# New orders of steps for a fused attention and mixture-of-experts layer, and one wait of TensorE moved

## What is computed

```
xn = layernorm(x)
s  = attention(xn)          # 16 heads of 8; 4 heads causal over all keys, 12 over a window of 32
y  = sum over 16 experts of act(xn) * cw @ Wd, plus one shared expert of width 128
g  = silu(xn + y)           # cw: top 4 of 16 experts, out of 2 of 4 groups, by sigmoid of xn @ gate_w
out = x + s * g
```

## Time and profile before

| | |
|---|---|
| median of three runs | 529.96 us |
| profiled execution, its time | 530.82 us |
| its span (first to last instruction) | 529.0 us |
| PE busy | 480.5 us (91%) |
| DVE busy | 340.3 us (64%) |
| ACT busy | 330.3 us (62%) |
| POOL busy | 265.9 us (50%) |

### The profile page before, as it was taken

The page is one execution under the profiler, slowest core; times in us unless marked ns, Lnnn a source line. Parts: engine busy times, 40 slices in busy tenths (PEclk is TensorE's granted clock), DMA queues, the critical chain, the costliest instruction groups (busy, mean ns, idle before and its releaser), DMA issues.

```text
span 529.0 us, 10545 instructions
## 1 busy us (share of the span) xinstructions
PE 480.5 (91%) x3804; PEld 289.0 (55%) x3832; DVE 340.3 (64%) x755; ACT 330.3 (62%) x654; POOL 265.9 (50%) x239
## 2 busy tenths in 40 slices
PE   1969988999999988999999998999999987989995
PEld 0756655555457655555446765555456755544442
DVE  6876464885687555777588474877588532686415
ACT  3456744767957544666957546566967556266972
POOL 3227851265736952155745972155744962016623
PEclk9979998999999999999999999999999999899999
DMA  9256383000350575000360396000260187000001
GB/s 216 80 164 115 58 103 64 1 1 2 124 76 0 165 96 82 1 1 1 93 109 0 91 162 89 2 0 1 82 119 2 48 156 97 2 2 0 1 1 40
DMA packets 144077, 32.37 MB, mean 61 GB/s; under 512 B 120966, under 2 KB 136346, under 8 KB 144026
## 3 DMA queue, kind: packets, MB, share of 16 engines
q1 hardware_dynamic: 143696, 31.41, 30.2%
q10 hardware_dynamic: 330, 0.30, 0.3%
HBM read 22.25 MB, written 9.44 MB: 60 GB/s over the span
## 4 chain that ended last, share of the span: by engine, by line
PE 72%; DVE 9%; ACT 6%; issue 6%; SPq 2%; POOL 2%; DMA 1%; POOLq 1%; DVEq 0%; ACTq 0%
PE bank L791 10%; PE bank L739 7%; PE bank L678 6%; PE bank L572 6%; PE bank L574 6%; PE bank L573 6%; PE bank L708 5%; DVE mxp L1176 4%; PE bank L755 4%; PE bank L779 3%; ACT stage L936 2%; PE bank L690 2%; PE bank L720 2%; PE bank L646 2%; PE bank L662 1%
## 5 line engine op out<-in xcount | busy, mean ns | idle before, releaser
L936 ACT ACTIVATE stage<-bank 128x512 f32<-128x512 f32 (+3 forms) x240 | 112.5, 528 | 62.0 <-PE bank L720 32.2
L1253 POOL TENSOR_TENSOR wrow<-wrow,gates 128x512 f32<-128x512 f32 x64 | 82.1, 1283 | 97.1 <-ACT wrow L865 96.9
L1176 DVE TENSOR_REDUCE mxp<-bank 128x1 f32<-128x512 f32 (+4 forms) x192 | 90.3, 518 | 41.1 <-PE bank L681 32.8
L1262 POOL TENSOR_TENSOR hid<-hid,wrow 128x512 f32<-128x512 f32 x64 | 81.8, 1278 | 37.1 <-DVE hid L1140 31.9
L1140 DVE SCALAR_TENSOR_TENSOR hid<-hid,bank 128x512 f32<-128x512 f32 x72 | 48.7, 680 | 60.0 <-PE bank L574 39.9
L791 PE MATMUL bank<-hid,down_w 128*128 128x512 f32 x144 | 77.8, 629 | 0.0
L854 ACT ACTIVATE hid<-bank 128x512 f32<-128x512 f32 x72 | 43.3, 602 | 51.1 <-PE bank L574 50.9
L1245 POOL TENSOR_TENSOR maxd<-mxp,k 128x512 f16<-128x512 f32 x32 | 33.4, 1048 | 79.7 <-DVE mxp L1176 45.7
L678 PE MATMUL bank<-kall,qpad 128*128 128x512 f16 (+4 forms) x192 | 54.0, 331 | 12.6 <-issue 6.8
L572 PE MATMUL bank<-xh,up_hi 128*128 128x512 f32 x144 | 58.3, 405 | 0.0
L708 PE MATMUL bank<-kpad,kall 128*128 128x512 f16 (+3 forms) x192 | 55.3, 330 | 2.0 <-ACT stage L936 0.6
(11 more groups left out here) (158 smaller groups left out, 884.4 us busy)
## 6 DMA issues: line engine op xcount, KB each, us to landing
planes<-qkh SPq DMA_DIRECT2D x16, 256.0 KB, 3.1
qtmp<-planes SPq DMA_DIRECT2D x16, 256.0 KB, 3.2
kall<-planes SPq DMA_DIRECT2D x16, 256.0 KB, 3.5
qpad<-planes SPq DMA_DIRECT2D x128, 32.0 KB, 2.9
kpad<-planes SPq DMA_DIRECT2D x48, 64.0 KB, 3.3
xin<-in_L_attn_x_dram SPq DMA_DIRECT2D x4, 512.0 KB, 4.6
planes<-qkl SPq DMA_DIRECT2D x8, 256.0 KB, 3.0
xres<-in_L_attn_x_dram SPq DMA_DIRECT2D x4, 512.0 KB, 4.1
```

The lines of the kernel that those rows point to most:

```text
L936: act.activation(prob[:, t % NPROB, 0:cols], ps[:, 0:cols], ACT.Exp).then_inc(freed, 1)
L1176: ins = dve.tensor_reduce(mxp[:, c, j:j + 1], ps[:, 0:cols], AX_X, ALU.max)
L1253: pool.tensor_tensor(row, row, gates[:], ALU.mult).then_inc(gated, 1)
L1262: pool.tensor_tensor(hid[:, i % NHID, :], hid[:, i % NHID, :], wrow[:, (EP * c + t) % NWT, :] if t < EP else gates[:], ALU.mult)\
```

## The change

The three strings are replaced; each has as many of every letter as before. And PE's wait for `k32` moves from the step `small` to a place ahead of FIRST, since `small` is no longer PE's first step. No instruction is added or taken away but that wait.

```diff
-FIRST_ORDER = ("IPIPIPPIPIITTPIIPTTTPPVITTPIVIITTIXXXXIVPPPVPPVXXVPXXIXPVPPVXPXXVVXXX")
+FIRST_ORDER = ("PPIPPIPIIPPTITIPITTIIIITTIVPTPVTTPXXVVVXXVIXIVPXPXIXXPVPPPPPVPXVXXXXX")
...
                     elif kind == "small":
-                        pe.wait_ge(k32_loaded, 16)
                         pe.wait_ge(small_loaded, 5 * 16)
...
+            pe.wait_ge(k32_loaded, 16)
             sections(pe, walk)
```

More of the change, by code:

```diff
@@ L151, in expert_steps @@
     return out
-FIRST_ORDER = ("IPIPIPPIPIITTPIIPTTTPPVITTPIVIITTIXXXXIVPPPVPPVXXVPXXIXPVPPVXPXXVVXXX")
[L155 to L161, removed]
+FIRST_ORDER = ("PPIPPIPIIPPTITIPITTIIIITTIVPTPVTTPXXVVVXXVIXIVPXPXIXXPVPPPPPVPXVXXXXX")
+BODY_ORDER = ("AAAXRRRXAPRXXXAAAAAAAXRXAAARARPRAAXAAAAARXAXRRRRRAAAAARRRAAAAAAAARAAAAAAXAAAXRRRRXAPRAXXAAAARRRA"
+              "AAAARAAXRRARARARRRARAAAXXRARRRARRAPRAAXARRRRRXRRAAPAXAAXRRRRRXAAARRRRRRAAXRAPPAXRRPRXRRRXRXRTRRR"
+              "RRPRRTPRRRRRXRRTXRRRXXRPRRRRXRXRRRRRPPTRCTRXTXRRRRXRXCRRPRXTPRRRRPPRRRRRRRRXRXXPRRRRRXRTTRPCXXVX"
+              "V0XVC0VXVXVXV1V1VXXP0X1VXXXXX")
+LAST_ORDER = ("AAXXARRRRRAXAXXAARRXAARAAAARAXAXAAARRARAARRXAAAARARRAAAAAAAAAAAAAAXAAAXARAXRRRAAXARARRARARRAAAAA"
+              "RXAXARAARARARARRRRAARRAAAARXAAXARAXARXARAXAAAXAARRRRRRRXRRRXRRRRRRRRAAXRXRXRRXRRRRXXRRRRRRRRRRRX"
+              "RCRRRXRRRRRRCRRRRXRRRRRRRRXRRRRRRXRRXRRRRRRRRRRRRRRRRRXRXXX0XCCX0X1X011")
 FIRST_EXPERTS = expert_steps(0) + [("z", 0), ("z2", 0)]
```

## The result

The changed kernel takes 534.99 us (median of 20 runs, 531.30 to 538.55), the kernel before 530.99 in the runs beside it. It is slower by 4.0 us in the medians, within the 1% that was called "the same". The ratio of the runs beside each other is 1.0093, 95% interval 1.0071 to 1.0115; it is not that of the two medians and makes 3.8 to 6.1 us. Ratios leave out executions in the chip's slower state, of which there is one of `kpads12_act_old_head` and one of the kernel before. 533.3 was forecast. The profiled execution took 534.31 us with a span of 532.5, against 530.82 and 529.0.

The account below looks back on a forecast made before the run. PE is busy for 91% of the span, so only its waits and clock can change the time; `cwT`'s start sets FIRST's end. Span 529.0 + 4.0 (FIRST) - 0.7 (LAST) = 532.3, carried to the median 533.3 us; range 526.5 to 537.5.

Parts of the forecast that it names:

- Load and `gate`: Start of FIRST: `x` lands 0.7 us earlier, but ACT's constants fall between its two copies, so `gate` starts 1.7 later.
- DVE's stand behind `route 0`: FIRST's routing: DVE idles about 1.6 us for ACT's first `up_hi`; with `gate` and the split, `route 1` starts 3.9 later.
- Behind it: FIRST, from `route 1` to `cw`: more splits cost about +0.9 us, less loss to POOL gives -0.8.
- The term for POOL: FIRST's routing chain: DVE may lose 0.8 us less, since POOL's work on `q 0` falls while DVE stands.
- rival D: FIRST: late `k 1` delays strips; `max 0 0` lacks pads if they land after about 54; up to 4 us, chance 0.13.
- Behind `cwT`: FIRST, from `cwT` to the first score: same steps in another order, 21.58 us, sum unchanged: 0.
- The clock: FIRST around `cwT`: PE's slow clock already costs about 1.1 us; longer idling could double it, making FIRST +5.1.
- BODY and LAST: Four later stretches to `max 3`: set by SP's queue, so 0 from reordering, each 25.5 to 28 us; LAST's maxima -0.7.
- LAST's -0.7: LAST, group 3's maxima: `times 1 0` leaves DVE there, saving a third of 2.6 us of waiting.
- B: Rival: FIRST does not get later, as PE's work behind `cwT` or DVE's stand is better filled; 529.3 us, chance 0.20.
- C: Rival: moved work covers the waits, all four later stretches take 25.6 us or less; -5.8 in all, chance 0.17.
- A: The forecast itself: FIRST later by 2.5 to 5.5 us, the rest unchanged; 531.5 to 536, chance 0.50.

Follow-up runs that it names:

- kpads12_act_old_head: Changed kernel with groups 1 and 2's `kpads` transfers on ACT's queue and FIRST's first 33 steps in the old order: 527.15 us, ratio 0.9953 to the kernel before.
- old_first_nine: Changed kernel with FIRST's first nine steps as before, the others in the new order; ran once, no ratio: first score at 59.35 us (changed kernel 62.08).
- k1_early: Changed kernel with `q 1` and `k 1` moved right behind `route 3`; ran once, no ratio: first score at 61.58 us (changed kernel 62.08).
- max_late: Changed kernel with `v 1 1`, `v 1 2` and `v 1 3` moved ahead of `max 0 0`; ran once, no ratio: first score at 62.26 us (changed kernel 62.08).
- head_old_tail_new: Changed kernel with FIRST's first 33 steps (head, to `cwT 1`) old and the 36 behind them (tail) new: ratio 1.0023 to the kernel before.
- kpads_cut: Changed kernel with each `kpads` transfer cut to 4 of 32 blocks; ran once, no ratio: four stretches to `max 3 0` sum to 98.5 us (changed kernel 109.5).

## Why the prediction was right, and where its steps were off

The total was right to 1.7 us and FIRST to 0.4 (+4.36 against +4.0). The path, x to `cwT`, and the waits on it were right. That FIRST came out so near is luck: two of its terms were mis-sized, by -1.4 and +1.5, and cancelled.

- **Load and `gate`**: right. `stats` starts 0.48 earlier (-0.7 forecast), `gate` 1.81 later (+1.7). The constants end at 16.8 (16.6). `old_first_nine` shows that the place of `setup`, `small` and the clearings is the cause; that the constants make most of it is read from the timeline of ACT.
- **DVE's stand behind `route 0`**: right. 1.52 (1.6), and `route 1` begins 4.17 later (+3.9).
- **Behind it**: mis-sized, +0.1 forecast, -1.34 measured (14.01 from `route 1` to `cw` before, 12.67 after). The further splits cost 0.8, as forecast (0.9). The term for POOL, "-0.8, an estimate", should have been -2.1. Before, all four of POOL's subtractions lay beside this chain. The later three in POOL's timeline of before:

```profile
26.46 2.44 POOL L1235 TENSOR_TENSOR qkl<-sT,qkh 128x512 f16<-128x512 f32 x2 [1.64 <-ACT qkh L924]
30.67 1.15 POOL L1235 TENSOR_TENSOR qkl<-sT,qkh 128x512 f16<-128x512 f32 x1 [1.77 <-ACT qkh L924]
```

  And what DVE has beside them, in its timeline of before:

```profile
26.48 1.28 DVE L964 TENSOR_TENSOR msk<-msk,gm 128x128 f32<-128x128 f32 x1
29.73 2.24 DVE L964 TENSOR_TENSOR pre<-pre 128x128 f32<-128x128 f32 x4
```

  After, `msk` takes 0.29 and the four `pre` 1.38. POOL's timeline of after, behind `q 0`:

```profile
27.65 1.15 POOL L1235 TENSOR_TENSOR qkl<-sT,qkh 128x512 f16<-128x512 f32 x1 [1.84 <-ACT qkh L924]
39.36 2.32 POOL L1235 TENSOR_TENSOR qkl<-sT,qkh 128x512 f16<-128x512 f32 x2 [10.56 <-ACT qkh L924]
```

  That `q 0` falls into DVE's stand was seen. That `q 1` and `k 1`, which rival D found too late for the pads, leave DVE's chain for the same reason was not; putting them back lengthens it by 0.84 (`k1_early`). By the lengths of the operations held up, the -2.1 is about 0.6 for `q 0` (0.8 forecast), 1.0 for `q 1` and `k 1`, and 0.6 for `k 0`, which held up `msk` for 1.0 before and a `cmp` at 28.23 for 0.4 after (0.72 in place of 0.29). The last is chance: `max_late` has the same 33 steps, and there `k 0` meets another `cmp` and costs 0.9.
- **Behind `cwT`**: mis-sized, 0 forecast, +1.53 measured. "Their sum does not change" failed: PE's waits grow by 2.17 (1.16 to 3.33) and its work falls by 0.64. The waits are 1.9 for the pads and 0.9 for `cwT`, whose copies stand behind `k 1`'s on ACT. `head_old_tail_new` shows that both come from the head, and `k1_early`, where neither is left, that they come from the late `q 1` and `k 1`. This is rival D, whose bound was "later than about 54", with the pads "at 51". PE was at `max 0 0` by 52.2; the last write of `planes` was issued at 43.69 (41.5), the strips at 48.07 (44.5), the last pads at 53.4, and PE waited till 53.6 for the first and 55.4 for the second half.
- **The clock**: the further 1.1 did not come; it went the other way. Before, behind the wait of 4.13 the granted clock is at the lower level, and the eight transposes of `cwT` take 1.88:

```profile
33.53:36.14 2.61, 2.61 (x11) 2.16 (x11) 2.14 (x8) 0.60 (x1) 0.00 (x0) 0.50 0.78 265
```

  After, PE works without a break from 33.05 to `cwT`, whose transposes take 1.04. The same new tail has 20.95 us of PE's work behind the old head at a granted 0.95, and 19.78 behind the new one at 1.00: 1.17 came back, the 1.1 that the prediction called "paid already". Against the old tail's 20.42 it shows as 0.64, since the new tail has 0.5 more at the same 0.95. The rule of the Trainium skill ("TensorE: Matmul & The Clock Gate", Part 1) agrees with this, and with `k1_early`; what was wrong was to hold the later `cwT` for longer idling just ahead of it.
- **BODY and LAST**: right. The stretches stay between 26.6 and 28.1, `kpads_cut` shows why, and the three BODY sections are 0.3 us shorter together. LAST's -0.7 was -0.6, but not for the reason given: in its maxima the waits shrank by only 0.24 (2.63 to 2.39), the rest is within the spread of the runs.
- **The rivals**: B and C did not come. A did, with a part of D in it. The range's lower end, 526.5, is not C's upper case as it says (527.5); the result does not hang on it.

## What to carry to other kernels

A step that is moved takes along its work on every engine: `q 1` and `k 1`, moved to the end of the routing, freed DVE of POOL (0.8 to 1.0 us), kept PE's clock up, and made the pads and `cwT` late (2.9 us of PE's waits). Where a stretch is as long as a queue's transfers, cut what they carry before reordering the work: with an eighth of `kpads`' bytes 11 us came back (in a kernel that computes less than is asked), with a new order of steps none. Constants belong into the time in which the first load is awaited; between two links of the first chain, with what moved beside them, they cost 2.6 of their 3.0 us. And a start in one profiled execution is worth no more than its spread over executions of the same steps, here 0.6 to 0.7 us.

## What was not expected of the hardware

DVE's operation on two tiles of SBUF, the memory that the engines share, that begins while POOL subtracts ends just behind POOL's: begun at 24.50, 26.91, 31.57 and 26.48 it took 1.13, 1.22, 1.23 and 1.28 in place of 0.29, and in the first two cases ended 0.14 and 0.15 behind POOL's end. A split, which reads a bank of TensorE's results and one tile, was not held up: in the changed kernel it begins at 25.16, inside POOL's 24.64 to 25.80, and takes its usual 0.69. The Trainium skill ("SBUF — State Buffer", SBUF: two separate sides) says that the two share a pair of ports that one holds for its whole instruction; the traces agree. So it is not the share of POOL's time that counts but which operation starts inside it: the same 33 steps gave `cwT` at 38.97 and, in `max_late`, at 39.33.

The granted clock of the records and the spacing of the matmuls differ early in FIRST. For the stretch ahead of `cwT` the records of the changed kernel show 1.00 (columns as above):

```profile
29.00:38.97 9.97, 7.16 (x30) 6.11 (x29) 8.43 (x35) 4.17 (x9) 0.00 (x0) 1.00 0.00 0
```

Its matmuls of `q 1` and `k 1`, 512 columns each, in PE's timeline:

```profile
36.93 0.63 PE L573 MATMUL bank<-xh,wqk_lo 128*128 128x512 f32 x1
37.35 0.63 PE L574 MATMUL bank<-xl,wqk_hi 128*128 128x512 f32 x1
...
38.06 0.39 PE L573 MATMUL bank<-xh,wqk_lo 128*128 128x512 f32 x1
38.30 0.40 PE L574 MATMUL bank<-xl,wqk_hi 128*128 128x512 f32 x1
```

The first two start 0.42 apart, which is 1.2 columns per ns, the last two 0.24, which is 2.1. PE had worked without a break since 33.05. I take the spacing for the better witness, since the recorded 1.00 does not change where the spacing nearly halves; by it the changed kernel, too, reached the higher level only just ahead of `cwT`.
